# Attention scores on all rows of their head, and normalisation factors for two chunks at once, in a four-layer graph kernel

## What is computed

```
xl, xr = x @ Wl, x @ Wr ; ee = edge_attr @ We        (each as heads x channels)
z      = leaky_relu(xl[src] + xr[dst] + ee, 0.2)
score  = einsum('ehc,hc->eh', z, att)
a      = exp(score - segment_max(score, dst)[dst])
out    = segment_sum(xl[src] * a / segment_sum(a, dst)[dst], dst)
```

## Time and profile before

| what | before |
|---|---|
| median of 3 runs | 9635.66 us (9634.32 to 9646.82) |
| the profiled execution's own time | 9562.17 us |
| its span | 9560.3 us |
| TensorE busy, instructions | 5960.4 us (62%), 15032 |
| VectorE busy | 6713.4 us (70%), 20701 |
| ScalarE busy | 2831.8 us (30%), 6861 |
| GpSimd busy | 4490.4 us (47%), 4367 |
| mean granted clock of TensorE | 0.618 of full speed |

### The profile page before, as it was taken

How to read it: one execution, slowest core, us unless ns; L and a number is a source line. 1 busy time by engine, 2 the same in 40 slices (tenths; PEclk the granted TensorE clock), 3 DMA queues, 4 the chain that set the end, 5 groups by cost and what they waited for, 6 DMA issues and landing times. The chain is left out here.

```text
span 9560.3 us, 99896 instructions
## 1 busy us (share of the span) xinstructions
PE 5960.4 (62%) x15032; PEld 2923.7 (31%) x15032; DVE 6713.4 (70%) x20701; ACT 2831.8 (30%) x6861; POOL 4490.4 (47%) x4367
## 2 busy tenths in 40 slices
PE   0006999996999997776000889867869999800000
PEld 0002333332444444664000446723323333300000
DVE  2677888885666665887555898867869999877422
ACT  0002333331111112554333000134434444346300
POOL 1775555554555553554554000055556666313466
PEclk9998555555656665555555897578855555555555
DMA  4002334432222221111333002566633333322222
GB/s 146 1 1 44 56 56 56 56 56 50 47 47 47 46 47 28 36 37 44 85 88 80 5 4 67 150 109 130 128 67 74 72 74 73 81 89 110 79 82 78
DMA packets 937356, 627.70 MB, mean 66 GB/s; under 512 B 649081, under 2 KB 811542, under 8 KB 935760
## 3 DMA queue, kind: packets, MB, share of 16 engines
q1 hardware_dynamic: 580324, 305.65, 12.4%
q0 software_dynamic: 137984, 138.92, 11.8%
q10 hardware_dynamic: 218920, 181.82, 5.8%
HBM read 431.25 MB, written 228.04 MB: 69 GB/s over the span
## 5 line engine op out<-in xcount | busy, mean ns | idle before, releaser
L722 POOL DMA_INDIRECT a_xg<-t_XL,a_ix x784 | 785.5, 1002 | 668.3 <-issue 647.5
L722 POOL DMA_INDIRECT b_xg<-t_H,b_ix x784 | 783.3, 999 | 668.1 <-PE b_bank L932 379.6
L722 POOL DMA_INDIRECT g_xg<-t_D,g_ix x784 | 825.8, 1053 | 527.7 <-issue 227.4
L1762 POOL DMA_INDIRECT f_dg<-t_D,f_ix x392 | 383.9, 979 | 1291.1 <-DMA f_ix<-t_PSRC 1163.7
L1105 POOL DMA_INDIRECT t_RANK<-m_place,m_at x392 | 384.5, 981 | 415.0 <-DMA m_place<-t_POS 307.3
L1290 POOL DMA_INDIRECT l_d<-t_D,l_ix x392 | 370.8, 946 | 401.7 <-DVE l_xs L1306 234.1
L2177 POOL DMA_INDIRECT out<-o_y,o_ix x392 | 386.6, 986 | 230.9 <-issue 198.7
L1380 PE MATMUL pr_prow<-c_ident,pr_col 128*1 128x128 f32 x2 | 0.6, 394 | 786.0 <-DVE pr_col L1398 786.0
L445 POOL DMA_INDIRECT t_XL<-ix_pv,ix_si x392 | 407.9, 1041 | 160.0 <-issue 137.7
L760 DVE TENSOR_TENSOR b_zt<-b_xl,b_bank 128x512 f32<-128x512 f32 x98 | 67.4, 687 | 550.9 <-issue 210.2
L1339 ACT ACTIVATE l_hn<-l_xs,l_sm 128x64 f32<-128x64 f32 x784 | 265.0, 426 | 501.7 <-issue 259.6
(11 more groups left out here) (439 smaller groups left out, 17014.5 us busy)
## 6 DMA issues: line engine op xcount, KB each, us to landing
t_XL<-in_nodes ACTq DMA_DIRECT2D x10, 2578.1 KB
t_XSD<-a_xg SPq DMA_DIRECT2D x98, 256.0 KB
t_H<-a_oE ACTq DMA_DIRECT2D x98, 256.0 KB
l_xb<-t_XSD SPq DMA_DIRECT2D x49, 512.0 KB
f_rl<-t_REL SPq DMA_DIRECT2D x49, 512.0 KB
g_xb<-t_XSD SPq DMA_DIRECT2D x98, 256.0 KB
n_x<-in_x SPq DMA_DIRECT2D x39, 640.0 KB
out<-n_y ACTq DMA_DIRECT2D x39, 640.0 KB
```

What stands on the lines that cost most here:

```text
L722: nc.gpsimd.indirect_dma_start(xg[k][:, j, i, :], None, table, bass.IndirectOffsetOnAxis(ap=ix[k][:, i, j:j + 1], axis=0)).then_inc(s_g[k] ...
L1762: nc.gpsimd.indirect_dma_start(dg[k][:, u, j, :], None, T["D2"], bass.IndirectOffsetOnAxis(ap=ix[k][:, u, j:j + 1], axis=0)).then_inc(s_g[ ...
```

## The change

`att1r`, `att2r`, `att3r` are the attention vectors with each head's column repeated for all rows of that head (for layer three, twice over, so that it fills 128 rows). The score product thus gives a head's score on every row of the head, and START, the maximum, the exponents and both weights are held on 128 partitions. The `factors` products and their 0/1 matrices are gone; `sums` reads the weights from SBUF and waits for `exponents` itself. In layer three the 64 upper rows carry the bare weights through the same scan (`both`), so that the denominator's scan is gone. In layers one and two the denominator is turned by four transposes like the sums'. In layer two, the second half's transposes get a PSUM bank of their own.

In layers one and three `norm` runs for odd chunks alone, for that chunk and the one before: statistics of both, then the 18 factor operations once on 16 columns. L is 4 instead of 3; `norm` is at L - 3, `normed` at L - 2, and SyncE's `extras` and `starts` at L - 2. In `logit_block` there are four slots instead of three, and `logits` and `store` have lag 3 instead of 2. The diff, cut to its core:

```diff
-        L = 2 if wide else 3
+        L = 2 if wide else 4
...
+        both = R < P
...
-        bT, bZ, bX, bS, bF0, bF1, bF2, bO = (m.ps(f"bank{b}", [P, CH]) for b in range(8))
+        bT, bT2, bZ, bX, bS, bD, bO = (m.ps(f"bank{b}", [P, CH]) for b in range(7))
...
-                sp.dma_start(start[k][:, :], line(T["START"], n, H)).then_inc(s_start[k], 16)
-            flow(sp, [(0, indices), (1, extras), (1, starts)], slots=SL)
+                sp.dma_start(start[k][:, :], line(T["START"], n, P)).then_inc(s_start[k], 16)
+            flow(sp, [(0, indices), (L - 2, extras), (L - 2, starts)] if not wide else [(0, indices), (1, extras), (1, starts)], slots=SL)
...
-            ch1 = Chain(dve, S["ch1"], 1 + LN_OPS + (tag == "g"))
+            ch1 = Chain(dve, S["ch1"], 2 + LN_OPS + 2 * (tag == "g"))
...
             def norm(n, k, q, old):
-                ch1.at(n)
-                dve.wait_ge(s_g[k], NG * (q + 1))
-                if tag == "g":
-                    dve.wait_ge(s_xb[k], 16 * (q + 1))
-                    ch1(v.tensor_tensor(xg[k][:, :, :, :], xg[k][:, :, :, :], xb[k][:, :, :, :], ALU.add))
-                ch1(row_moments(nc, xg[k][:, :, :, 0:D].rearrange("p j s d -> p (j s) d"), bn))
-                if later(n):
-                    dve.wait_ge(S["hn"], n)
+                if k % 2 == 0:
+                    return
+                ch1.at(2 * q + k // 2)
+                for h, c in enumerate((k - 1, k)):
+                    dve.wait_ge(s_g[c], NG * (q + 1))
+                    if tag == "g":
+                        dve.wait_ge(s_xb[c], 16 * (q + 1))
+                        ch1(v.tensor_tensor(xg[c][:, :, :, :], xg[c][:, :, :, :], xb[c][:, :, :, :], ALU.add))
+                    ch1(row_moments(nc, xg[c][:, :, :, 0:D].rearrange("p j s d -> p (j s) d"), bn[:, h * PG:(h + 1) * PG, :]))
+                if later(n, 2):
+                    dve.wait_ge(S["hn"], n - 1)
                 norm_factors(nc, ch1, bn, sm, S["ln"])
                 ch1.done()
 
...
-                sc = bS[0:H, :]
+                sc = bS[:, :]
...
             def sums(n, k, q, old):
                 ch4.at(n)
-                dve.wait_ge(S["b"], n + 1)
+                dve.wait_ge(S["ex"], n + 1)
                 dve.wait_ge(S["xl"], n + 1)
-                ch4(v.tensor_tensor(msg[:, :], bF1[0:R, :], xl[k][:, :], ALU.mult))
                 if later(n):
                     dve.wait_ge(S["sum"], n)
+                weighted = ex[k][0:R, 1, :] if both else msg[:, :]
+                ch4(v.tensor_tensor(weighted, ex[k][0:R, 1, :], xl[k][:, :], ALU.mult))
                 if old:
                     dve.wait_ge(S["o"], n - SL + 1)
-                v.tensor_tensor_scan(num[k][:, :], bF0[0:R, :], msg[:, :], num[(k - 1) % SL][:, CH - 1:CH],
-                                     ALU.mult, ALU.add).then_inc(S["sum"], 1)
+                v.tensor_tensor_scan(num[k][:, :], ex[k][:, 0, :], ex[k][:, 1, :] if both else msg[:, :],
+                                     num[(k - 1) % SL][:, CH - 1:CH], ALU.mult, ALU.add).then_inc(S["sum"], 1)
                 ch4.done()
 
             def quotients(n, k, q, old):
...
-                v.reciprocal(recT[k][:, :], bF2[:, 0:J * H]).then_inc(S["rec"], 1)
+                weights = (bO if both else bD)[:, :].rearrange("p (j r) -> p j r", j=J)[:, :, (R if both else 0)::R // H]
+                v.reciprocal(recT[k][:, :, :], weights).then_inc(S["rec"], 1)
...
-                stages = [(L, leaky), (L + 2, quotients), (L + 1, denominator), (L + 1, sums), (L, maximum), (L - 2, norm)]
+                stages = [(L, leaky), (L + 2, quotients), (L + 1, sums), (L, maximum), (L - 3, norm)]
+                if not both:
+                    stages.insert(2, (L + 1, denominator))
...
-                act.wait_ge(S["ln"], n + 1)
+                act.wait_ge(S["ln"], 2 * q + k // 2 + 1)
...
-                    act.wait_ge(S["b"], n - SL + 1)
-                    act.wait_ge(S["den"], n - SL + 1)
+                    act.wait_ge(S["sum"], n - SL + 1)
+                    if not both:
+                        act.wait_ge(S["den"], n - SL + 1)
...
-                stages = [(L, values), (L, features), (L - 1, normed), (L - 1, turned), (L, exponents), (L + 2, results)]
+                stages = [(L, values), (L, features), (L - 2, normed), (L - 1, turned), (L, exponents), (L + 2, results)]
...
-                mm(bS[0:H, :], att[:, :], zt[k][:, :], start=True, stop=True).then_inc(S["s"], 1)
-
-            def factors(n, k, q, old):
-
-                pe.wait_ge(S["ex"], n + 1)
-                if later(n):
-                    pe.wait_ge(S["sum"], n)
-                mm(bF0[0:R, :], sel[:, :], ex[k][:, 0, :], start=True, stop=True)
-                mm(bF1[0:R, :], sel[:, :], ex[k][:, 1, :], start=True, stop=True).then_inc(S["b"], 1)
+                mm(bS[:, :], att[:, :], zt[k][:, :], start=True, stop=True).then_inc(S["s"], 1)
 
             def results(n, k, q, old):
-                hold(pe, S["pturn"], (S["sum"], n + 1), (S["den"], n + 1))
+                hold(pe, S["pturn"], (S["sum"], n + 1))
+                if not both:
+                    hold(pe, S["pturn"], (S["den"], n + 1))
                 if later(n):
                     hold(pe, S["pturn"], (S["oE"], n))
                 for j in range(J):
-                    tr(bO[:, j * R:(j + 1) * R], split(num[k][:, :])[:, :, j], C["ident"][0:R, 0:R])
-                if wide:
-
-                    hold(pe, S["pturn"], (S["h"], min(n + 3, NCH) if isinstance(n, int) else n + 3))
-                for j in range(J):
-                    last = mm(bF2[:, j * H:(j + 1) * H], split(den[k][:, :])[:, :, j], C["ident"][0:H, 0:H],
-                              start=True, stop=True)
+                    last = tr(bO[:, j * P:(j + 1) * P], split(num[k][:, :])[:, :, j], C["ident"][:, :])
+                    if not both:
+                        last = tr(bD[:, j * P:(j + 1) * P], split(den[k][:, :])[:, :, j], C["ident"][:, :])
                 last.then_inc(S["o"], 1)
-            stages = [(L, project), (L + 1, factors), (L, scores), (L - 1, turn), (L + 1, results)]
+            stages = [(L, project), (L, scores), (L - 1, turn), (L + 1, results)]
             flow(pe, stages, slots=SL)
...
+            for name, heads, again in (("att1", 8, 1), ("att2", 2, 1), ("att3", 4, 2)):
+                att = C[name + "b"]
+                rows_ = att.shape[0]
+                width = P // (heads * again)
+                for g in range(again):
+                    v.tensor_copy(C[name + "r"][:, :].rearrange("p (g h c) -> p g h c", g=again, c=width)[:, g, :, :],
+                                  bcast(att[:, :], width))
...
-        SL = 3
+        SL = 4
...
+                if later(n):
+                    dve.wait_ge(s_e, n)
...
-            flow(dve, [(2, logits), (1, norm)], total=NB, slots=SL)
+            flow(dve, [(3, logits), (1, norm)], total=NB, slots=SL)
...
-            flow(act, [(2, store), (1, normed)], total=NB, slots=SL)
+            flow(act, [(3, store), (1, normed)], total=NB, slots=SL)
```

72 lines of the change are left out of this document (33 added, 39 removed).

## The result

The changed kernel takes **10149.88 us** (median of four, 10130.41 to 10162.59), the kernel before 9637.83 us beside it: a ratio of **1.0528**, 95% interval 1.0509 to 1.0547. The forecast was 10010 us with a range up to 10120: the direction and most of the size were right, and the time lies 30 us above the range.

The account below looks back on a forecast made before the run. TensorE's work was taken as the bound, then waits by order. Layers one to three +300, -111, +382, logit block -211, filling +25: together +385 on 9562, 9947; as median 10010, range 9770 to 10120.

Parts of the forecast that it names:

- the first circle: Layers one and three: norm, normed, turned, project, leaky, sums wait in a ring; 17.8 us a chunk against 14.71, 17.0 against 13.06.
- the 35.5 of the sum: Layer one: the ring's links added up for one pair of chunks, 35.5 us, so 17.8 us a chunk.
- the logit block at 10.8: Logit block: VectorE and ScalarE no longer take turns; 10.8 us a batch against 15.2, for 48 intervals, -211 us.
- the collision on POOL's side: Logit block: POOL's descriptors stretched while VectorE reads two SBUF operands; bounds 0 and 2.5 us a batch, taken as 0.9.
- The rule cited in the prediction: GpSimd's SBUF interfaces are shared with VectorE, contended by two-SBUF-input instructions; in full, logit block 12.4 us a batch, 77 us more.
- The circle of the earlier trace: Layer two: project's start to sums' end 11.35, results 2.24, then next project: 13.6 us, taken as 13.2 against 14.34.
- rival (1): TensorE's clock rises to 2.4 GHz in the circles: sum -362 us, 9275; chance 0.09 in full or most, 0.03 half.
- The second circle: TensorE: results waits for the same step's sums and the next project is queued behind it; layer two 13.2 us a chunk.
- POOL's floor: Layer two, should TensorE's clock rise: held by POOL's eight descriptors at about 10.4 us a chunk.
- The fills: Layers one and three: one step more of filling, 2 x 12 = 25 us.
- No circle: An order was read wrongly and engines overlap as before: layers 15.0, 13.2, 10.5 us; -517 us, 9120; chance 0.04.
- Rival (3): START's copies or stretched descriptors make the gather late in both odd steps: up to +200, 10200; chance 0.10.

Follow-up runs that it names:

- e3: Kernel before with only the pair's norm and its lags (L = 4, norm at lag 3, normed at lag 2): 10194 us beside 9239.
- e1: Changed kernel with the pair's factors made a step earlier (L = 5, two buffers of statistics and factors): 8416 us beside 9239; later 9515 beside 9635.
- p1: Kernel before with only the pair's norm, but L = 5, normed at lag 3 and two buffers of statistics and factors: 9731 us beside 9642.
- run 197: Not a run's number: 197 of 735 small operations started late in the logit block of the changed kernel's first run, 10150 us beside 9638.
- l_half: Changed kernel with four of eight columns gathered in the logit block: 9.34 us a batch in both series; 9288 us beside 9243, 9989 beside 9635.
- after_again: Changed kernel run again unchanged, in the faster series: 9366 us beside 9244, ratio 1.0131.
- p3: Changed kernel loading START's 128 copies twice, the second set into a spare buffer: 10178 us beside 9642, ratio 1.0531.
- e2: Changed kernel with the norm made per chunk as before (L = 3, normed at lag 2): 8773 us beside 9239.

## Why the prediction was right, and where it wasn't

**Right, the first circle.** Layers one and three became slower because the factors are made in the step in which they are used. The forecast for layer one was 17.8 and for layer three 17.0; measured were 18.12 and 17.58, and 16.81 and 16.74 without the long gaps. e3 has the loss without the scores' half, e1 takes it away, p1 does both. The split was right as well: VectorE idles 8.91 us in one step and 2.8 to 4.0 in the other, for the 9 and 4 foreseen. Most pairs of layer one took 34.2 us in the run without gaps, for the 35.5 of the sum. Nearly all of that is one term: the second project of a pair was priced at 4.65 us and took 3.5 there, partly at the upper clock level. That the first comparison met the forecast to 0.3 us is in part luck, then: the gaps put back what this term had too much.

**Wrong, the term that put the time outside the range: the logit block at 10.8.** It took 13.00, which is 106 us over the block's 48 intervals. The step that failed is "VectorE needs 15.2 - 5.6 = 9.6 us a batch": it takes VectorE's small operations as 0.2 us apart, as nearly all of them were in the kernel before. In the changed kernel's first run 197 of 735 started over 0.3 us late, up to 2.6 us, and VectorE's row came to 13.0 us a batch. The step holds where nothing starts late: 9.34 us a batch in l_half, 10.88 in after_again. The cause of the late starts stays open; shown is that they come in the series at 9640 us alone, and hardly any with four descriptors a batch. The kernel before had shown 43 late starts in its trace, 15 of them in this block, and the prediction does not speak of them. I looked for the collision on POOL's side (descriptors stretched by VectorE, 0.9 us). The rule cited in the prediction from the Trainium skill, "GPSIMD Engine Reference", 1. Specifications, gave 12.4, nearer to 13.00 in the first comparison, but the second has 10.88 with the same instructions; and the descriptors took 0.98 us where the block took 13.00 and 1.02 where it took 10.88, so it is not by that stretching that the block was slow. That layers one and three passed their forecast by 0.3 and 0.6 us (31 and 56 us) goes with the late starts as well, since without them both stayed below it.

**Wrong in size, layer two.** 13.2 was forecast, 12.50 came (-67 us), and 11.43 without late starts. The circle of the earlier trace rows was priced mostly at the lower level. The granted clock rose from 0.61 to 0.71: the part of rival (1) that concerns layer two came true in part, in layer two alone. The second circle was there, at 0.5 to 0.7 us. POOL's floor is close beneath it: by its group in after_again, eight descriptors of 1.075 us with 0.30 ahead of each take 11.0 of the 11.43 us.

```profile
L714 POOL DMA_INDIRECT b_xg<-t_H,b_ix x784 | 842.7, 1075 | 325.9 <-issue 229.1
```

**Right in sum by luck, in part.** The logit block's and the layers' excess and layer two's shortfall have opposite signs. In the second comparison nothing hides the latter: +385 us would be 9629, and 9366 was measured, 263 less. There the direction is right and the size is not, by some 170 us in layer two and 100 in layer one.

**Smaller.** The fills were 62 us and not 25. TensorE was expected near 60% busy in layer one and was 47%. By the steps, the profiled execution was missed by 115 (logit block, 10 of it from 15.2 for 15.0) + 31 + 56 - 67 + 37 = 172 of the 200 us between 9947 and 10147; stages outside the change give the rest. The median of the kernel before lay 74 above its profiled execution and that of the changed kernel 3 above, which took some of the miss away again.

**The rivals.** No circle and the risen clock are out for layers one and three: TensorE is 47% and 44% busy there, at a clock of 0.54 and 0.50. Rival (3), up to 10200, had the right time for a reason that p3 doesn't bear out (START) and e2 does only in part (stretched descriptors).

## What to carry to other kernels

When an operation is batched over two steps, count at which step its result is first asked for: half of the users now ask in the step that makes it, and one more step of lag and a second buffer (e1) may be the difference between +1.3% and -9%, or between +5.3% and -1.2% in the slower series. A row of small chained operations that other engines wait for can cost far more in one series than in another; read the idle time ahead of each such operation, in more than one run, before a price is put on the row. And where a kernel's own time differs between series, compare steps, not totals, and measure a change beside its own kernel before in more than one series.

## What the runs showed of the hardware that was not expected

- In the series with the kernel before at 9640 us, engines start late now and then: VectorE's chained operations of 0.17 us up to 2.6 us behind the last one's end (197 of 735 in the changed kernel's logit block, 6 of 735 with half of the gather's descriptors), ScalarE, in the case shown, 4 us behind the product that it waits for in layer two. In the ten runs of the other series no chained operation of this kind started more than 0.3 us late, not even beside an unbroken row of GpSimd's descriptors.
- The same kernel before took 9240 or 9640 us by series while its layers' steps agreed to 0.1 us, and the change's effect was +123 or +512 us by the same division.
- TensorE's granted clock was 0.52 while it was 94% busy in layer one of the kernel before, 0.54 at 47% in the changed kernel, and 0.75 at 55% in e1. In layer three it was 0.50 in all of them, 67% busy in e1. The Trainium skill, "TensorE: Matmul & The Clock Gate", Part 1, lets activity release the clock; busy time alone does not order these rows.
